# VectorE's dependent steps set apart in its queue, two decay groups bounded by minima, a new order for the first phase

## The reference, cut to what matters

```python
x = x + mamba(_layernorm(x))            # 32 heads of 16, state of 128
#   dt = softplus(dt_in + dt_bias);  A_bar = exp(-exp(A_log) * dt)
#   h = A_bar*h + (dt*B) x;  y = C.h + Dp*x
#   y = rmsnorm(y)*norm_w * silu(z);  out = y @ out_proj
x = x + xattn(_layernorm(x), ctx)       # 16 heads of 16, keys masked
x = x + moe(_layernorm(x))              # 16 experts, the 2 best, one shared
```

## Time and profile before

| | |
|---|---|
| time, median of 3 runs | 4331.63 us (4328.83 to 4337.89) |
| profiled execution, its own time | 4321.73 us |
| its span, first to last instruction | 4320.1 us |
| mean granted clock of TensorE | 0.946 |
| busy: PE, DVE, ACT, POOL | 93%, 78%, 66%, 52% |

### The profile page before, as it was taken

One profiled execution on the slowest core, in us unless ns is written; L12 is line 12 of the kernel. 1 busy time (PEld: TensorE's weight loads), 2 busy tenths in 40 slices (PEclk: granted clock), 3 DMA queues, 4 the chain that ended last, 5 costly groups with the idle time before them and its releaser, 6 DMA issues.

```text
span 4320.1 us, 118128 instructions
## 1 busy us (share of the span) xinstructions
PE 4024.4 (93%) x34582; PEld 3103.4 (72%) x34583; DVE 3366.7 (78%) x8730; ACT 2840.8 (66%) x7282; POOL 2233.6 (52%) x2996
## 2 busy tenths in 40 slices
PE   5999999999999999997997999999999999999998
PEld 4777877787788777875775666666666666666665
DVE  4888888888888888884554777878787877778776
ACT  4777877787787777774443666666565666566664
POOL 3555555555555555551223555555555555555554
PEclk9898889899999999987998999999999999999999
DMA  3333332323323323232441001010111111111110
GB/s 124 123 103 120 97 123 88 104 90 104 108 89 105 108 87 106 87 104 70 146 144 47 29 29 33 27 35 27 34 30 31 30 31 30 31 32 29 30 31 20
DMA packets 222642, 304.14 MB, mean 70 GB/s; under 512 B 57216, under 2 KB 176256, under 8 KB 222592
## 3 DMA queue, kind: packets, MB, share of 16 engines
q1 hardware_dynamic: 197632, 249.83, 18.5%
q0 software_dynamic: 19200, 52.45, 3.7%
q10 hardware_dynamic: 5760, 1.24, 0.2%
HBM read 239.18 MB, written 64.23 MB: 70 GB/s over the span
## 4 chain that ended last, share of the span: by engine, by line
PE 68%; DVE 18%; issue 8%; ACT 3%; DVEq 1%; DMA 1%; POOL 1%; ACTq 1%; POOLq 0%; SPq 0%
PE Q L1481 18%; PE Q L1474 16%; PE Q L1486 10%; PE Q L1509 4%; PE Q L1515 4%; PE Q L1845 3%; PE Q L1878 3%; PE Q L1697 3%; DVE arena L872 2%; PE Q L1524 2%; DVE arena L825 2%; PE Q L1709 2%; DVE rt L992 1%; DVE sel L977 1%; ACT arena L1196 1%
## 5 line engine op out<-in xcount | busy, mean ns | idle before, releaser
L1486 PE MATMUL Q<-ident,arena 128*128 128x128 f32 x3872 | 647.8, 290 | 119.0 <-ACT arena L1204 38.2
L1486 PEld LDWEIGHTS Q<-ident,arena 128*128 128x128 f32 x3872 | 464.1, 147 | 285.1 <-issue 138.3
L640 POOL TENSOR_TENSOR arena<-arena 128x1024 f32<-128x1024 f32 x256 | 488.7, 1924 | 69.3 <-DMA arena<-cum_rows 68.4
L1481 PE MATMUL Q<-Wkvl,arena 128*128 128x512 f32 x1024 | 499.6, 600 | 0.0
L705 POOL TENSOR_TENSOR l<-l,half_pow 128x8 f32<-128x8 f32 x192 | 318.5, 1659 | 231.1 <-DVE l L1083 229.2
L1325 ACT ACTIVATE arena<-Q,mx 128x128 f32<-128x128 f32 x1024 | 277.9, 382 | 210.3 <-DVE mx L909 210.3
L1474 PE MATMUL Q<-arena,Win 128*128 128x128 f32 x2560 | 373.9, 293 | 1.5 <-DVE arena L853 1.1
L730 POOL TENSOR_TENSOR arena<-arena,part_of 128x512 f32<-128x512 f32 x256 | 263.7, 1041 | 195.8 <-DVE part_of L1121 195.8
L1474 PEld LDWEIGHTS Q<-arena,Win 128*128 128x128 f32 x2560 | 340.1, 204 | 32.9 <-issue 25.7
L1515 PE MATMUL Q<-ident,arena 128*128 128x128 f32 x2048 | 308.9, 286 | 16.3 <-ACT arena L1325 13.4
L872 DVE TENSOR_TENSOR arena<-arena,Q 128x1024 f32<-128x1024 f32 x256 | 311.8, 1218 | 7.7 <-ACT arena L1271 7.0
(11 more groups left out here) (291 smaller groups left out, 10419.9 us busy)
## 6 DMA issues: line engine op xcount, KB each, us to landing
arena<-cum_rows SPq DMA_DIRECT2D x256, 512.0 KB, 6.5
arena<-routed_rows SPq DMA_DIRECT2D x144, 128.0 KB, 2.0
expert_rows<-arena POOLq DMA_DIRECT2D x144, 128.0 KB, 2.0
arena<-in_x_dram SPq DMA_DIRECT2D x128, 128.0 KB, 4.5
arena<-in_ctx_dram SPq DMA_DIRECT2D x128, 128.0 KB, 2.1
x_rows<-arena SPq DMA_DIRECT2D x128, 128.0 KB, 1.7
arena<-x_rows SPq DMA_DIRECT2D x128, 128.0 KB, 2.1
out_dram<-arena SPq DMA_DIRECT2D x64, 128.0 KB, 1.7
```

The costliest lines, as they stand in the source:

```text
L640: tell(g.tensor_tensor(E8[j], E8[j], cums[:, 8 * j:8 * j + 8].unsqueeze(2).broadcast_to([P, 8, T]), ALU.subtract), "diff")
L1481: last = mm(out, lhs(c), rhs(c), start=c == 0, stop=c == n - 1)
L1486: last = nc.tensor.transpose(out[:, c * P:(c + 1) * P], src[:, c * P:(c + 1) * P], ident[:, :])
```

## The change

It has four parts. `link` is split, on VectorE in the first phase, into `cue`, which issues with an increment, and `heed`, which waits; between the two there is now a `yield`, so that the order may put other steps there. The chains M, W, F, D, V, P and G are cut in this way; within `Gsb` the product of the slots no longer waits for the update of `base`. Second, in groups 0 and 1 of the decay weights ScalarE's absolute value is gone: VectorE takes the minimum with zero (`Nc0`, `Nc1`), and ScalarE the exponential of that. Groups 2 and 3 stay. Third, `ORDER[1]` is new for SP, DVE, ACT and PE; POOL's is the same. Fourth, SyncE loads the context one pass earlier (lag 1, not 2). What is computed for the tokens that count is the same.

```diff
     1: {
         "SP": """
-            Yc Ncb0 Mx Ncb1 Ncb2 Ncb3 Gm Ox Xm Dco Go
+            Ncb0 Mx Ncb1 Ncb2 Xm Ncb3 Gm Go Yc Ox Dco
...
         "DVE": """
-            Mln1 Wln2 Gtop Gslot Nm0 Zgz Yk Ghg Ddt Nm1 Dsp Dsp6 Dsp4 Dsp2 Gxo Dsp0 Pho Nm2 Fln3 Nm3 Vcv1 Oy Vcv2 Xm0 Xm1 Oss Vcv3 Fr Vxs2 Xm2 Xm3
-            Vxdt Bcb Ox1
+            Mln1 Mln1v Gtop Wln2 Gwt Nc0 Gslot Gsb Wln2v Nc1 Nm0 Gsn Zgz Ddt Nm1 Yk Dsp Dsr Dss Dsz Ds7 Ds6 Ds5 Ds4 Ds3 Ghg Ds2 Ds1 Ghh Ds0 Nm2 Dsd
+            Pho Dsa Phm Gxo Nm3 Phx Fln3 Fln3v Vcv1 Oy Xm0 Xm1 Vcv2 Oss Fr Vcv3 Fri Frs Vxs2 Frb Xm2 Xm3 Vxdt Bcb Ox1
         """,
         "ACT": """
-            YcT Ne0 Pt0 Nf0 Ne1 Ztz Mln1 Nf1 Gth Mln1n Pt1 Pt2 Dab Ne2 Pt3 Wln2 Xmr POT Yv Nf2 Ne3 Wln2n Nf3 Vcv Dcum Wq Bbc Fln3 Fln3n Xm0 Xm1 Vcth
-            Frx Xm2 Xm3
+            Pt0 Pt1 Pt2 Ne0 Mln1 YcT Ztz Mln1n Ne1 Dab Pt3 Ne2 Dae Nf2 Yv POT Gth Wln2 Ne3 Nf3 Wln2n Vcv Dcum Xmr Wq Fln3 Fln3n Xm0 Bbc Xm1 Vcth Frx
+            Xm2 Xm3
         """,
         "PE": """
-            YcT Pt0 Zz Yk Yv Zzh Pt1 Ggu Gguh Mln1n Pt2 Ddt Pt3 Ppv Gdn Ppv0 Ppv1 Ppv2 Ppv3 Vip1 POT Vip1h Wln2n Nv0 Wq Dcum Nv1 Nv2 Nv3 Bbc Xs0 Fln3n
-            BCB Fr Oss Opr Xs2 Oprh VxsT Frk
+            Pt0 Zz Pt1 Pt2 Zzh YcT Pt3 Ppv Ppv0 Ppv1 Mln1n Yk Ddt Yv Ggu Ppv2 Ppv3 Gguh Vip1 Vip1h Wln2n POT Gdn Dcum Wq Nv0 Nv1 Nv2 Nv3 Xs0 Fln3n Bbc
+            Fr Oss Opr Xs2 Oprh VxsT BCB Frk
         """,
...
+        def cue(name, ins):
...
+            ins.then_inc(SEM[f"link_{name}"], 1)
...
+        def heed(eng, name, b, bare=False):
...
+            eng.wait_ge(SEM[f"link_{name}"], at(f"link_{name}", b, steps[name]))
...
             def moments(n, src, st, mv, c, b):
-                link(dve, c, b, v.bn_stats(st[:, :], src), bare=True)
+                cue(c, v.bn_stats(st[:, :], src))
+                yield f"{n}v"
+                heed(dve, c, b, bare=True)
                 tell(v.bn_aggr(mv[:, 0:2], st[:, :]), f"{n}_var")
...
             def N(b):
+                for j in (0, 1):
+                    if j == 0:
+                        yield "c0"
+                        done(dve, "diff", b, 1)
+                        tell(v.tensor_scalar(Ew[j], Ew[j], 0.0, None, ALU.min), "cap")
+                    if j == 1:
+                        yield "c1"
+                        done(dve, "diff", b, 2)
+                        tell(v.tensor_scalar(Ew[j], Ew[j], 0.0, None, ALU.min), "cap")
...
                 yield "ab"
                 done(act, "dt_pre", b)
                 tell(s_.activation(dts[:, 1, :], dts[:, 0, :], ACT.Abs), "dt_abs")
+                yield "ae"
                 done(act, "dt_abs", b)
...
                 yield "e0"
-                done(act, "diff", b, 1)
-                tell(s_.activation(Ew[0], Ew[0], ACT.Abs), "gap")
-                yield "f0"
-                done(act, "gap", b, 1)
-                tell(s_.activation(Ew[0], Ew[0], ACT.Exp, scale=-1.0), "E")
+                done(act, "cap", b, 1)
+                tell(s_.activation(Ew[0], Ew[0], ACT.Exp), "E")
```

More of the change, by code:

```diff
@@ L296, in two_layers @@
         signals("O", "POOL", "sq yg rms")
-        for n, k in (("gap", 4), ("E", 4)):
+        for n, k in (("gap", 2), ("cap", 2), ("E", 4)):
             sig(n, k)
@@ L360, in link @@
             ins.then_inc(SEM[f"link_{name}"], 1)
+            eng.wait_ge(SEM[f"link_{name}"], at(f"link_{name}", b, steps[name]))
+            if bare:
+                eng.sem_inc(SEM[f"passed_{eng.engine.name}"], 1)
+        def cue(name, ins):
+            steps[name] += 1
+            assert steps[name] <= links[name], name
+            ins.then_inc(SEM[f"link_{name}"], 1)
+        def heed(eng, name, b, bare=False):
             eng.wait_ge(SEM[f"link_{name}"], at(f"link_{name}", b, steps[name]))
@@ L805, in M @@
                 done(dve, "xa_in", b, 16)
-                moments("ln1", xa, stM, mvM, "M_DVE", b)
+                yield from moments("ln1", xa, stM, mvM, "M_DVE", b)
             def D_(b):
-                J = lambda ins, bare=False: link(dve, "D_DVE", b, ins, bare)
+                J = lambda ins: cue("D_DVE", ins)
                 yield "dt"
@@ L842, in V @@
                     if shift < NCONV - 1:
-                        J(last)
+                        cue("V_DVE", last)
                     else:
@@ L901, in W @@
                 done(dve, "x1", b)
-                moments("ln2", x1, stX, mvX, "W_DVE", b)
+                yield from moments("ln2", x1, stX, mvX, "W_DVE", b)
             def X(b):
@@ L964, in F @@
             def F(b):
-                J = lambda ins, bare=False: link(dve, "F_DVE", b, ins, bare)
                 yield "ln3"
                 done(dve, "x2", b)
-                moments("ln3", x2, stF, mvF, "F_DVE", b)
+                yield from moments("ln3", x2, stF, mvF, "F_DVE", b)
                 yield "r"
@@ L972, in F @@
                 logits, top = Q[7][:, D:D + NE], rt[:, 3, 0:8]
-                J(v.max(top, logits), bare=True)
-                J(v.max_index(rti[:, 0, :], top, logits))
+                cue("F_DVE", v.max(top, logits))
+                yield "ri"
+                heed(dve, "F_DVE", b, bare=True)
+                cue("F_DVE", v.max_index(rti[:, 0, :], top, logits))
+                yield "rs"
+                heed(dve, "F_DVE", b)
                 tell(v.tensor_scalar(rt[:, 0, 0:1], top[:, 0:1], -1.0, None, ALU.mult), "rmax")
@@ L977, in F @@
                     last = v.scalar_tensor_tensor(sel[:, k, :], iota[:, :], rti[:, 0, k:k + 1], ones[:, 0:NE], ALU.is_equal, ALU.mult)
-                J(last)
+                cue("F_DVE", last)
+                yield "rb"
+                heed(dve, "F_DVE", b)
                 tell(v.tensor_tensor(selb[:, :], sel[:, 0, :], sel[:, 1, :], ALU.add), "sel")
             def G(b):
-                J = lambda ins, bare=False: link(dve, "G_DVE", b, ins, bare)
+                J = lambda ins: cue("G_DVE", ins)
                 yield "top"
```

56 lines of the change are left out of this document (39 added, 17 removed).

## The result

The changed kernel takes 4185.65 us in the median of 4 runs (4182.89 to 4200.94), the kernel before 4334.76 beside it on the same chip: a ratio of 0.966, 95% interval 0.9628 to 0.9692, or 149 us less.

What follows compares the result with a forecast made beforehand. VectorE's timeline in the first phase was taken as the bound, over TensorE. A pass of 30.25 + 0.1 = 30.35 against 30.03, +0.3 x 62 = +19 us on 4331.6, gave 4350; range 4250 to 4425.

Steps and rivals of the forecast that it cites:

- Where the minima stand: Head of the pass: slot product still behind GpSimd's third subtraction, `Nc1` priced at 1.7, `Nm0` at 6.40, 2.16 later.
- rival 1: Minima not stopped by GpSimd: `Nm0` at 4.85, pass 29.0, -1.0 x 62 = 4270 us; chance 0.30.
- I weigh 0.7 to 0.3: Tail of the pass: `Frb` loses to GpSimd's second subtraction (0.7, pass 30.75) or wins (0.3, 29.1), giving 30.25.
- Waits taken out: VectorE chains: 15 of 28 waits covered, five at 0.23 and ten at 0.11, 2.25 us of issue time.
- buys nothing: Router chain: first and last covered short waits precede a step stalled for GpSimd anyway, so 0.3 gains nothing.
- TensorE: `Bbc` moved into the narrow stretch and `BCB` behind `VxsT` should make the lower clock rarer in the pass's tail.
- I add 0.1 for what remains: Tail on TensorE: 0.1 us a pass added for tail steps that still run at the lower clock.
- Minima added: `Nc0` and `Nc1` on VectorE: 0.69 each, 0.61 from start to start, 1.22 together; ScalarE loses two absolutes of 1.1.
- alone is worth nothing: ScalarE's two saved absolutes of 1.1 gain nothing alone, since VectorE does not wait for ScalarE in this stretch.
- From `Nm0` to `Oss`: Middle of the pass: VectorE needs 16.4 instead of 18.39, but TensorE has `Oss` ready at 22.95, 0.3 later than before.
- The row DMAs: SyncE: `Dco` near 17.8, first wide load 19.3, 0.5 later; second load makes the second subtraction meet `Frb`; other loads free.
- The rivals: Set after the result against the main theory: gain is TensorE's alone, the minima's, or the row DMA order's; no chances given.

Runs made afterwards that it cites:

- Experiment 1: Changed kernel, new order kept, VectorE again waiting at once behind each of the 28 steps: 4541.81 us with doubled waits, 4443.74 with single waits (`Nm0` at 6.70).
- experiment 2: Changed kernel with part of the waits at once back: in the body alone 4309.43 us, in two places of the head alone 4299.74 us.
- Its second kernel: Changed kernel with a wait at once in only two places, behind the ln2 moments and behind the reciprocal in `Gtop`: 4299.74 us, ratio 0.9928.

## Why the prediction was wrong

**The step that failed: "Where the minima stand".** It said that `Nc0` "holds GpSimd's last small step a little, so the third subtraction starts near 2.25", with the slot product at 2.39 behind it. It had the moment right (1.44 forecast, 1.37 measured), the length right (0.69), the slot product nearly right (2.27), and the exclusion right. It took GpSimd's power step as finished or untouched. In fact that step was running, was held for 0.46, and put the subtraction at 2.55. The order of two events forecast 0.14 us apart came out the other way, by 0.28, and with it a chain: the slot product 0.18 instead of 1.77, `Nc1` 0.67 instead of about 2.3, `Nm0` at 3.61 instead of 6.40. The forecast and its rival 1, which had `Nc1` free but `L992` still caught, both hung on this margin of 0.14, and no rival had the slot product ahead of the subtraction; that was the place for a far wider bound. Experiment 1 shows the other side of the margin, with `Nm0` at 6.70.

What this step was worth, experiment 2 shows. Its second kernel is close to the forecast in the head: slot product 1.83, `Nc1` 2.34, `Nm0` at 6.69, and `Oss` at 22.98 where 22.95 was forecast. It takes 4299.74. So the head is about 114 of the 164 us, and 50 are something else. Even with this head the kernel is 35 us faster than the one before, so the direction was wrong for another reason as well.

**The second step, "I weigh 0.7 to 0.3".** The prices of the tail were good: a pass of 30.75 was forecast if `Frb` is caught and 29.1 if not, and in that kernel most passes that are caught take 30.65, and most others 28.9 to 29.1. But of its 43 passes between 500 and 1800 us only 16 are caught by the second subtraction, 12 at `Frb` and 4 at the selection: 0.37, not 0.7. (0.7 - 0.37) x 1.65 x 62 = 34 us, an estimate from these numbers; for the remaining 16 the cause is open.

**Waits taken out.** The prices stand in the sum: 1.38 for the nine between `Dsp` and `Oss`, against 1.35 by 0.11 and 0.23. That 0.3 of the router chain's "buys nothing" wasn't tested. What the prediction didn't see is the head: there two waits are worth 1.84 a pass, not 0.34, because they decide who comes first. The Trainium skill, "VectorE: DVE Perf Modes", section "The DRAIN you can't avoid", has separation gain nothing; the 1.38 speak against it here, in a stretch where no step of VectorE takes more than 0.05 us longer than in the changed pass, so none stands still for GpSimd.

**TensorE.** That the move of the wide columns should leave the lower clock rarer was right. It is worth 72/62 = 1.2 us a pass in the kernel before, and 1.8 in the new order, and no term of the sum says so: the new pass was built up from durations and set against the mean pass of 30.03, which contains the slow passes. The term "I add 0.1 for what remains" isn't contradicted: with the head as forecast and a granted clock of 0.98, the passes that aren't caught take no longer than forecast.

**Minima added.** The length was right (0.69). That ScalarE's saving "alone is worth nothing" fits the kernel before, where the minima lose 55 us. In the new order it doesn't: without the minima `Zgz` waits 2.0 us a pass for ScalarE, and with them 61/62 = 1.0 us a pass is gained in all.

**From `Nm0` to `Oss`.** Right: 16.55 forecast (22.95 less 6.40), 1041.16 - 1024.33 = 16.83 measured. `Oss` waits 0.34, as said (no more than 0.5).

**The row DMAs.** `Dco` was forecast at 17.8 and the first load at 19.3; they stand at 15.34 and 17.16, earlier by most of the 2.79. The collision of `Frb` with the second subtraction, which the sum gave 0.7, is rare: L1024 takes 0.164 in the median and up to 1.87, and is held in 6 of 46 passes. Its price was right, its chance was not, as said. That the other loads cost nothing stands within what the runs can tell.

**The rivals.** Theory by theory: TensorE's clock is a real second part, but not all, since the waits alone are worth 258 us with that move in place; the minima are worth 61 in the new order and lose 55 alone; the order of the row DMAs is about 21, not clear of nothing. The parts don't add up to 149: what one is worth depends on which others are there, as the minima show.

**Open.** Why L639 is held by a minimum that began 0.28 us later, while a subtraction on GpSimd holds such a minimum to its end, no run here tells; the profile's times on GpSimd are rough, too. That the hold of L639 is what keeps the slot product free behind `Nc0` is read from the order of the steps in experiments 1 and 2: the kernels in which `Nc0` comes after the power step lose both. No run keeps L639 from being held and leaves the rest as it is. What sets the 16 us of the forecast's tail is open too.

## What to carry to other kernels

Where two engines exclude each other, the question at each meeting is who asks first: write down the margin of every such meeting, and where it is smaller than the error of the start times (here 0.14 us by the forecast, and 1.84 us a pass hung on it), forecast both outcomes and let the range hold both. Waits ahead of such a meeting are worth what they flip, the same waits elsewhere about their own length. A chance that multiplies a large price (here 0.7 of 1.65 us) is a term of the sum like any other and needs a row behind it. And one experiment with the forecast's own head tells how much of an error that step was; the difference in start times alone (2.79 x 62 = 173 us) would have made it the whole.

## What the runs showed of the hardware

- GpSimd's small power step on 128x1 (L639), 0.55 us alone, takes 1.01 when VectorE starts a minimum of 128x1024 0.28 us after it; the minimum keeps its 0.69. The step behind it (128x1, 0.28 alone) takes 0.67 beside one such minimum and 1.32 beside two. The Trainium skill, "SBUF — State Buffer", section "Who interferes with whom", gives the shared ports to whoever starts first, for the whole instruction. The subtractions agree (a minimum held to 2.09 and 2.34 us), this power step doesn't: it started first and was still held.
- The same nine waits between dependent steps on VectorE add 1.38 us to a stretch of 12.46, with the same instructions in the same order.
- Moving some 0.9 us of wide columns on TensorE by a few steps, with no change in what is computed, took the granted clock of two windows of 500 us from 0.92 to 0.97 and 0.94 in one kernel; undoing it took it from 0.97 to 0.88 and 0.87 in the other.
